# A tokenizer, state-space block and two MLPs on one core: norm factors straight from the variance, and another order at two turns

## The reference

```
h  = patches @ W.T + b
x  = layernorm(h)
m  = rmsnorm(x) * rms1_w ; zxbcdt = m @ in_proj.T       # z, x, B, C, dt
dt = softplus(dt_in @ dt_proj.T + bias)
h_t = exp(dt*A) * h_{t-1} + dt*x*B ; y = sum_n C*h_t    # 1024 channels, 16 states
y  = (y + D*x) * silu(z)
x1 = x + y @ out_proj.T
x2 = x1 + MLP(rmsnorm(x1) * rms2_w)
h  = h + x2 ; out = h + MLP2(layernorm(h))
```

## Time and profile before

| | |
|---|---|
| median of 3 executions | 671.52 us (671.13 to 671.97) |
| the profiled execution | 673.53 us |
| its span | 671.7 us |
| PE busy | 631.7 us (94%) |
| DVE busy | 417.6 us (62%) |
| POOL busy | 429.2 us (64%) |
| ACT busy | 345.1 us (51%) |
| mean granted clock of PE | 0.98 |

### The profile page before, as it was taken

One profiled execution on the slowest core, in us unless ns is written; L12 is line 12 of the kernel. 1 busy time (PEld: TensorE's weight loads), 2 busy tenths in 40 slices (PEclk: granted clock), 3 DMA queues, 4 the chain that ended last, 5 costly groups with the idle time before them and its releaser, 6 DMA issues.

```text
span 671.7 us, 8616 instructions
## 1 busy us (share of the span) xinstructions
PE 631.7 (94%) x2846; PEld 504.8 (75%) x2846; DVE 417.6 (62%) x532; ACT 345.1 (51%) x772; POOL 429.2 (64%) x244
## 2 busy tenths in 40 slices
PE   4959998799999899999998999999999999999998
PEld 3737765466666667777765777766999998999998
DVE  4077896889887889878898988850322223332132
ACT  4359789348888564334365433422543442653441
POOL 0176874527877999997879987644464463445461
PEclk9878998899999899999999999999999999999999
DMA  8699998369999959999967999534443353244421
GB/s 340 236 358 348 311 303 301 137 211 365 344 363 351 392 198 346 414 354 320 334 257 259 387 343 335 180 121 132 134 143 126 125 158 126 63 128 137 143 68 44
DMA packets 49165, 163.50 MB, mean 243 GB/s; under 512 B 4321, under 2 KB 18529, under 8 KB 48481
## 3 DMA queue, kind: packets, MB, share of 16 engines
q1 hardware_dynamic: 49120, 162.95, 69.5%
HBM read 145.24 MB, written 17.69 MB: 243 GB/s over the span
## 4 chain that ended last, share of the span: by engine, by line
PE 77%; DVE 12%; ACT 4%; issue 3%; DMA 2%; POOL 1%; SPq 0%; DVEq 0%; ACTq 0%
PE work L1001 55%; PE da L1001 15%; PE work L1011 6%; DVE da L790 6%; DVE hs L800 2%; ACT L525 1%; DMA bb<-b_rows 1%; ACT da L551 1%; DMA c_rows<-c_rows 1%; DMA sm<-small 1%; DVE sq L872 1%; DVE a L855 0%; POOL hs L450 0%; DVE sq L888 0%; DVE a L881 0%
## 5 line engine op out<-in xcount | busy, mean ns | idle before, releaser
L790 DVE TENSOR_TENSOR_SCAN da<-da,hs 128x580 f32<-128x580 f32 (+1 forms) x128 | 191.1, 1493 | 42.8 <-POOL hs L450 25.8
L450 POOL TENSOR_TENSOR hs<-dtx,bb 128x1160 f32<-128x1160 f32 (+1 forms) x64 | 171.2, 2677 | 63.6 <-PE work L1011 54.5
L429 POOL TENSOR_TENSOR ws<-wraw,ws 128x1024 fp32r<-128x1024 f32 x40 | 101.4, 2535 | 92.9 <-ACT ws L560 92.9
L1001 PE MATMUL work<-sq,wraw 128*128 128x290 f32 x512 | 127.0, 407 | 4.2 <-DVE gate L941 2.6
L1001 PEld LDWEIGHTS work<-sq,wraw 128*128 128x128 f32 x512 | 96.1, 189 | 34.8 <-issue 5.2
L1001 PE MATMUL work<-hn,win 128*128 128x290 f32 (+1 forms) x336 | 105.7, 465 | 16.8 <-DVE hn L863 8.1
L551 ACT ACTIVATE da<-dt,a_neg 128x261 f32<-128x261 f32 (+1 forms) x256 | 118.2, 493 | 0.0
L800 DVE TENSOR_TENSOR hs<-da,cb 128x580 f32<-128x580 f32 (+1 forms) x128 | 105.3, 823 | 10.4 <-DMA cb<-c_rows 2.5
L1001 PEld LDWEIGHTS work<-hn,win 128*128 128x128 f32 x336 | 66.8, 203 | 51.2 <-issue 27.1
L548 ACT COPY da<-zeros 128x58 f32<-128x58 f32 (+1 forms) x128 | 27.6, 216 | 125.7 <-DVE hs L800 125.5
L560 ACT CAST ws<-wraw 128x1024 fp32r<-128x1024 f32 x48 | 50.3, 1049 | 70.3 <-PE da L1001 34.4
(11 more groups left out here) (98 smaller groups left out, 649.3 us busy)
## 6 DMA issues: line engine op xcount, KB each, us to landing
wraw<-w_stream SPq DMA_DIRECT2D x104, 512.0 KB, 4.1
bb<-b_rows SPq DMA_DIRECT2D x32, 700.0 KB, 7.9
cb<-c_rows SPq DMA_DIRECT2D x32, 700.0 KB, 5.9
bb<-b_rows SPq DMA_DIRECT2D x32, 580.0 KB, 8.3
cb<-c_rows SPq DMA_DIRECT2D x32, 580.0 KB, 6.3
c_rows<-c_rows SPq DMA_DIRECT2D x8, 875.0 KB, 10.6
c_rows<-c_rows SPq DMA_DIRECT2D x8, 725.0 KB, 6.8
win<-w_in SPq DMA_DIRECT2D x4, 1024.0 KB, 13.0
```

What stands on the lines that cost most here:

```text
L429: nc.gpsimd.tensor_tensor(ws[:, k % NW, 1, :], wraw[:, split_loads[k] % NRAW, :], ws[:, k % NW, 0, :].bitcast(F32), ALU.subtract).then_inc ...
L450: nc.gpsimd.tensor_tensor(hs[:, u % NH, 0:NQ * n].rearrange("p (n t) -> p n t", t=n), dtx[:, t % 2, 0:n].unsqueeze(1).to_broadcast([P, NQ, ...
L790: nc.vector.tensor_tensor_scan(da[:, j, 0:w], da[:, j, 0:w], hs[:, u % NH, j * w:(j + 1) * w], 0.0, ALU.mult, ALU.add).then_inc(scan_done, 1)
L1001: last = nc.tensor.matmul(dst, w, x, start=(k == 0), stop=(k == len(pairs) - 1))
```

## The change

1. **Norm factors.** The RMS norm of the layer norm's output has the mean square var/(var+eps). With eps added and both roots taken together, the factor on the centred token is 1/sqrt(var (1+eps) + eps^2). ACT computes this first, as Exp(-0.5 Ln((1+eps) var + eps^2)), into the mean's bank, and DVE makes `hn` at once from the centred `a`. Then ACT computes the layer norm's own factor, and DVE scales `a` in the step `rms1`. The Exp to 1/(var+eps) and the DVE product on the variance are gone, and two semaphores with them.
2. **Tokens of chunk 1.** `tokc` becomes four steps `tok`. Their squares go, for chunk 1, into `th` and `acc` instead of `sq`; so the waits for `xs(0,7)` and for the stores of B move from the tokens to the steps that write `sq`. `in_z(0,7)` moves from slot 13 to slot 11; `in_c`, `dtp` and `xs` of tile 7 share slot 12, tokens go to slot 13, mean and variance to 14, `in_dt` and the first `in_b` to 15, and all of chunk 1's tiles come two slots sooner.
3. **Turn of the chunks.** `dtp(1,6)` and `xs(1,6)` come in slots 30 and 31, slot 32 is empty. In slots 30 to 32 PE does the state sum before the other steps, and sum(31) directly after sum(30). The last gate of chunk 0 comes in the middle of unit 33 on DVE instead of behind it.

```diff
-    slots = [(None, [("bmean", 0), ("tokc", 0), ("mean", 0), ...
+    slots = [(None, [("bmean", 0), *tokens(0), ("mean", 0), ...
...
-    bg += [[("dtp", 0, 7), ("in_c", 0, 7)], [("xs", 0, 7), ("in_z", 0, 7)]]
-    bg += [[("tokc", 1)], [("mean", 1), ("ln1", 1)], [("rms1", 1)], [("in_dt", 1), ("in_b", 1, 0)],
-           [("in_x", 1, 0), ("in_b", 1, 1)], [("in_x", 1, 1)]]
+    bg[-1].append(("in_z", 0, 7))
+    bg += [[("in_c", 0, 7), ("dtp", 0, 7), ("xs", 0, 7)], tokens(1), [("mean", 1), ("ln1", 1)],
+           [("rms1", 1), ("in_dt", 1), ("in_b", 1, 0)], [("in_x", 1, 0), ("in_b", 1, 1)], [("in_x", 1, 1)]]
     bg += two_tiles(1, 0) + two_tiles(1, 2) + two_tiles(1, 4)
     bg[-1].append(("in_z", 1, 6))
+    bg += [[("dtp", 1, 6)], [("xs", 1, 6)]]
-    first = [[("dtp", 1, 6), ("xs", 1, 6)], [("xs", 1, 7)], o[0:2], o[2:4]]
+    first = [[], [("xs", 1, 7)], o[0:2], o[2:4]]
...
+        def token_square(c, k):
+            if c == 0:
+                return sq[:, k, 0:TS[c]]
+            return (th[:, k, :] if k < 2 else acc[:, (k - 2) * TM:(k - 1) * TM])[:, 0:TS[c]]
...   (ACT, ln1)
-                    link(nc.scalar.activation(ln, bank(s), ACT.Ln, bias=eps_ap))
-                    nc.scalar.activation(inv, ln, ACT.Exp, scale=-1.0).then_inc(inverse_done, 1)
-                    act.wait_ge(h_done, KD * (c + 1))
-                    nc.scalar.activation(bank(("mean", c)), ln, ACT.Exp, scale=-0.5).then_inc(rstd_done, 1)
+                    link(nc.scalar.activation(both, bank(s), ACT.Ln, scale=1.0 + EPS, bias=eps_square))
+                    act.wait_ge(h_done, KD * (c + 1))
+                    nc.scalar.activation(bank(("mean", c)), both, ACT.Exp, scale=-0.5).then_inc(rstd_done, 1)
+                    link(nc.scalar.activation(ln, bank(s), ACT.Ln, bias=eps_ap))
+                    nc.scalar.activation(bank(s), ln, ACT.Exp, scale=-0.5).then_inc(rstd_done, 1)
...   (ACT, rms1)
-                    act.wait_ge(scaled_var, c + 1)
-                    link(nc.scalar.activation(rstd[:, 0:n], bank(var), ACT.Ln, bias=eps_ap))
-                    nc.scalar.activation(bank(var), rstd[:, 0:n], ACT.Exp, scale=-0.5).then_inc(rstd_done, 1)
+                    return
...   (ACT, in_dt, in_x, in_b)
+                    if c >= 1 and kind == "in_x":
+                        full(act, ("xs", c - 1, KI - 1))
+                    if c >= 1 and kind == "in_b":
+                        act.wait_ge(b_stored, 16 * 2 * c)
+                    if c >= 1 and kind == "in_dt":
+                        full(act, ("dtp", c - 1, KI - 1))
...   (DVE: ln1 now makes hn, rms1 scales a)
-                    nc.vector.tensor_tensor(bank(s), bank(s), rstd[:, 0:n], ALU.mult).then_inc(scaled_var, 1)
...   (DVE, order of a slot)
-                        parts.append(("gate", unit // QU - 1))
+                        parts.insert(2 if unit == UNITS + 1 else len(parts), ("gate", unit // QU - 1))
...   (PE, order of a slot)
-                n = 0 if unit is not None and unit % QU == 1 else (len(steps) + 1) // 2
+                n = 0 if unit is not None and (unit % QU == 1 or UNITS - 2 <= unit <= UNITS) else (len(steps) + 1) // 2
                 for s in steps[:n]:
                     step(s)
                 if unit is not None and 2 <= unit <= UNITS:
                     state_sum(unit - 2)
+                if unit == UNITS:
+                    state_sum(UNITS - 1)
                 for s in steps[n:]:
                     step(s)
-                if unit == UNITS:
-                    state_sum(UNITS - 1)
```

More of the change, by code:

```diff
@@ L90, in m_steps, with tokens @@
     return s
+def tokens(c):
+    return [("tok", c, k) for k in range(KD)]
 def outs(c):
@@ L104, in schedule @@
 def schedule():
-    slots = [(None, [("bmean", 0), ("tokc", 0), ("mean", 0), ("ln1", 0), ("rms1", 0), ("in_dt", 0), ("in_b", 0, 0), ("in_b", 0, 1),
+    slots = [(None, [("bmean", 0), *tokens(0), ("mean", 0), ("ln1", 0), ("rms1", 0), ("in_dt", 0), ("in_b", 0, 0), ("in_b", 0, 1),
                      ("dtp", 0, 0), ("in_c", 0, 0), ("in_x", 0, 0), ("xs", 0, 0)]),
@@ L166, in work_bank_uses @@
                 ring = RINGS[2]
-            names = {"tokc": [("tokc", s[1], k) for k in range(KD)], "rms1": [],
-                     "gu": [(s, "gate"), (s, "up")]}.get(s[0], [s])
+            names = {"rms1": [], "gu": [(s, "gate"), (s, "up")]}.get(s[0], [s])
             for n in names:
@@ L221, in build @@
         acc = sb("acc", [P, 2 * TM])
-        cols = sb("cols", [P, 8])
+        cols = sb("cols", [P, 9])
         zeros = sb("zeros", [P, 2 * TM // STEPS])
         eps_ap, w_sum, b_mean, minus_one, tok_bc = (cols[:, 0:1], cols[:, 1:2], cols[:, 2:3], cols[:, 3:4], cols[:, 4:8])
+        eps_square = cols[:, 8:9]
         with ExitStack() as scanned:
@@ L597, in step @@
                 n = TS[s[2] if kind in ("squares", "root") else c]
-                if kind == "tokc":
-                    if c == 0:
+                if kind == "tok":
+                    k = s[2]
+                    if (c, k) == (0, 0):
                         act.wait_ge(tokb_done, 1)
[L601 to L609, removed]
+                    full(act, s)
+                    nc.scalar.activation(a(c, k), bank(s), ACT.Identity, bias=tok_bc[:, k:k + 1]).then_inc(centered, 1)
+                    nc.scalar.activation(token_square(c, k), bank(s), ACT.Square,
+                                         bias=tok_bc[:, k:k + 1]).then_inc(free_of(s), 1)
@@ L610, in step @@
                 elif kind == "ln1":
-                    v, ln, inv = NORMS.index(s), rstd_ln[:, 0:n], rstd[:, 0:n]
+                    ln, both = rstd_ln[:, 0:n], rstd[:, 0:n]
                     log_tables()
-                    if v >= 1:
-                        act.wait_ge(norm_done, KD * v)
                     full(act, s)
+                    link(nc.scalar.activation(both, bank(s), ACT.Ln, scale=1.0 + EPS, bias=eps_square))
+                    act.wait_ge(h_done, KD * (c + 1))
+                    nc.scalar.activation(bank(("mean", c)), both, ACT.Exp, scale=-0.5).then_inc(rstd_done, 1)
@@ L770, in _ @@
             nc.vector.memset(minus_one, -1.0)
+            nc.vector.memset(eps_square, EPS * EPS)
             nc.vector.memset(zeros[:, :], 0.0)
@@ L850, in step @@
                 elif kind == "ln1":
-                    dve.wait_ge(inverse_done, c + 1)
-                    nc.vector.tensor_tensor(bank(s), bank(s), rstd[:, 0:n], ALU.mult).then_inc(scaled_var, 1)
-                    dve.wait_ge(rstd_done, NORMS.index(s) + 1)
+                    v, both = NORMS.index(s), ("mean", c)
+                    dve.wait_ge(rstd_done, v + 1)
+                    if c >= 1:
+                        full(dve, ("in_z", c - 1, KI - 1))
+                        full(dve, ("in_c", c - 1, KI - 1))
                     for k in range(KD):
-                        nc.vector.tensor_tensor(a(c, k), a(c, k), bank(("mean", c)), ALU.mult).then_inc(norm_done, 1)
+                        nc.vector.scalar_tensor_tensor(out=hn[:, k, 0:n], in0=a(c, k), scalar=small_ap(S_W1, k),
+                                                       in1=bank(both), op0=ALU.mult, op1=ALU.mult).then_inc(norm_done, 1)
+                    dve.wait_ge(norm_done, KD * (v + 1))
+                    dve.sem_inc(free_of(both), 1)
                 elif kind == "rms1":
@@ L858, in step @@
                     dve.wait_ge(rstd_done, v + 1)
-                    if c >= 1:
-                        full(dve, ("in_z", c - 1, KI - 1))
                     for k in range(KD):
-                        dve.wait_ge(norm_done, KD * (v - 1) + k + 1)
-                        nc.vector.scalar_tensor_tensor(out=hn[:, k, 0:n], in0=a(c, k), scalar=small_ap(S_W1, k),
-                                                       in1=bank(var), op0=ALU.mult, op1=ALU.mult).then_inc(norm_done, 1)
+                        nc.vector.tensor_tensor(a(c, k), a(c, k), bank(var), ALU.mult).then_inc(norm_done, 1)
                     dve.wait_ge(norm_done, KD * (v + 1))
                     dve.sem_inc(free_of(var), 1)
-                    dve.sem_inc(free_of(("mean", c)), 1)
                 elif kind == "rms2":
@@ L1050, in step @@
                     product(s, [(mean_w[:, :], sm[:, S_TOKB:S_TOKB + KD])], KD)
-                elif kind == "tokc":
+                elif kind == "tok":
                     pe.wait_ge(pat_loaded, 16 * (c + 1))
                     pe.wait_ge(tokw_done, 1)
-                    for k in range(KD):
-                        product(("tokc", c, k), [(tokw[:, k * P:(k + 1) * P], pat[:, OFF[c]:OFF[c] + n])])
+                    product(s, [(tokw[:, s[2] * P:(s[2] + 1) * P], pat[:, OFF[c]:OFF[c] + n])])
                 elif kind == "mean":
@@ L1058, in step @@
                 elif kind == "ln1":
-                    product(s, [(mean_w[:, :], sq[:, k, 0:n], free_of(("tokc", c, k)), uses[("tokc", c, k)][1] + 1)
```

(3 more changed lines are left out.)

3 lines of the change are left out of this document (removed).

## The result

| | before | after |
|---|---|---|
| median | 671.12 us (6 executions) | 664.73 us (6 executions) |
| ratio, 95% interval | | 0.9918 (0.9899 to 0.9938) |
| profiled execution | 673.53 us | 665.30 us |
| its span | 671.7 us | 663.5 us |

The change makes the kernel 6.4 us faster by the medians, 5.5 us by the ratio, with an interval of 4.2 to 6.8. The forecast was 10.0 us, 661.5. In the profiled executions it is 8.2 us. The difference between 8.2 and 6.4 lies mostly in the profiled execution of the kernel before: it took 673.53 us, while its executions in this study's four comparisons, 65 in all, have medians between 670.3 and 671.1 us.

The account below looks back on a forecast made before the run. TensorE (PE) was taken as three quarters of the chain of waits, its idles before full stretches paid in full. Turn 7.85, norm 1.84 and clock 0.3 gave 10.0 us: 673.5 to 663.5 profiled, median 661.5, range 657 to 668.

Parts of the forecast that it names:

- Part 1: First norm: a shorter chain from Ln to the first `hn` lets PE start 1.84 us sooner.
- The 0.3 for the clock: Behind the first norm's shorter gap, PE's clock may stay up, worth 0.3 us.
- Every step is a chain of dependent work: From the first norm on, the 1.84 us saved is carried through to the next turn.
- Part 2: Second chunk's tokens and norm sooner: unit 32 starts at 203.6 instead of 206.29, worth 2.7 us ahead of the turn.
- the 13.3 us of earlier `in_dt`: Second norm: PE starts `in_dt` at 117.0 instead of 130.28; 5.9 us of this is sums put behind it.
- The forecast of slower: Rival, chance 0.06: held-back sums free `hs` buffers late, costing 12.6 us against 10 gained, so 674.1 us.
- the larger last group of gates: On ACT, before unit 32: 1.3 us added to the time of the 14 units from 18.
- Part 3: Turn of the chunks: sums 30 and 31 first and gate 7 earlier, so `out(0,0)` starts at 212.3 instead of 221.65.
- I take 1.5: Turn: allowance of 1.5 us for unit 33's late `cb` load, between nothing and 7.0 us.
- Two signs of being wrong: Wrong if DVE waits for `cb` or POOL for `bb` in units 30 to 34, or gaps bring back half clock.
- I had taken 2.0 off for both: Whole kernel: the median taken as 2.0 us below the profiled time, giving 661.5 from 663.5.
- the loads set the turn: Rival, chance 0.13: unit 33's `cb` lands no sooner except by the norm's 1.84; gain 4.2 us, so 667.3.

Follow-up runs that it names:

- the run with chunk 0's norm alone: Kernel before with the new norm for chunk 0 only, chunk 1 keeping the old norm: 669.37 us, ratio 0.9978.
- the weights in slot 30: Changed kernel with its six first weight loads issued in slot 30, as before, instead of slot 28: 663.91 us, ratio 0.9899.
- one by one: Changed kernel with its six first weight loads in slots 29, 31, 33, 34, 35 and 36 instead of together in slot 28: 662.21 us, ratio 0.9873.
- the short norm alone: Kernel before with only the new norm factors, in both chunks; tokens, slots and turn as before: 665.90 us, ratio 0.9929.
- the slots alone: Kernel before with only the second chunk's earlier slots; both norms and the turn's orders as before: 677.47 us, ratio 1.0109.
- the short norm in the old slots: Kernel before with new norm, turn's orders and weight loads spread over slots 29 to 36: 660.96 us, ratio 0.9854; without the spreading 665.18 us.

## Why the prediction came out as it did

**Part 1, the chain.** Right to a few hundredths: 1.65 us from Ln to PE against 1.67, and 1.5 us of time in the run with chunk 0's norm alone against 1.84. The 0.3 for the clock was too little for the profile that the sum started from: there the clock's part is 7.79 - 6.10 = 1.7 us. The clock fell behind the old first gap in three of four profiles and behind the new one in none of ten. "Every step is a chain of dependent work" held only in part, since behind the norm the rows of B go out to DRAM and come back as `bb`. In the runs with the weights in slot 30 and one by one, which are alike up to there, that store was issued at 17.93 and 19.93 us, and unit 1's scan began at 38.29 and 38.26: POOL stood 5.01 us for its first `bb` in the one and 3.10 in the other. So 2 us of lead at the norm can be gone by unit 1. How much of the start's lead lasts to the end is open as well, since the run of chunk 0's norm, 6.5 us ahead at the output product, is 4.4 ahead at the end of its span.

**Part 2.** The sum was good as a description of the changed kernel. Shifted by the 4.1 us by which this execution was ahead at unit 12, it gives 103.6 for gate 2 (measured 104.2), 112.9 for `in_dt` (113.7) and 131.0 for unit 18 (131.8). It was wrong as an account of what earns it. I priced slots and second norm together and wrote the 13.3 us of earlier `in_dt` down to the slots. The runs show that the short norm alone reaches the same lead at unit 20 (8.3 against 8.2), that the slots alone lose 7.3 us, and on top of the norm nothing is gained. The forecast of slower, by sums that are held back, named a real mechanism. It decides when the norm is long: POOL then stood 12.97 us for sum(13). In the changed kernel only gate 2's wait for sum(11) is left of it, 2.58 us, where the sum had 2.4. And ACT had too small a price: the sum took 1.3 us for the larger last group of gates, but with the loads out of the way unit 32 is 2.9 us less ahead than unit 31.

**Part 3.** The multiply, the gate and the output product follow each other as forecast. The step that failed is "I take 1.5" for the loads. Measured by moving the weights it is 3.5 us at the output product: 213.46 against 209.95. My argument was that the landing would move with the weights. It took 184.84 to 200.4, still 15.5 us, but it now hit unit 31, whose multiply is due sooner than unit 33's. I had looked at the one load that was late before, not at which load would be next in line behind the bunch. PE's idle before the output product was 7.1 us, not 3 to 5, for the same reason. Two signs of being wrong that the prediction named did come: the waits for `cb` and `bb` in units 31 and 32, and the half clock behind the gap.

**The terms side by side,** as leads over the kernel before's profile in us. The last row is the changed kernel with its weights one by one.

```
             start to unit 12   to unit 32   to the output product   sum
forecast           2.1              2.7          5.2                10.0
changed kernel     4.1             -1.0          5.1                 8.2
weights late       4.0              0.9          6.8                11.7
```

The 5.2 is 6.7 less the 1.5 for the loads. From unit 32 on, the sum without loads was right to 0.1 us. Up to unit 32 it was 3.7 us too high: 1.9 for the loads, which hit there already, and 1.8 mostly for ACT. The start was 1.9 us better than forecast, of which the clock behind the first gap explains up to 1.7. So the 10.0 came as near to 8.2 as it did partly by luck: errors of +1.9 and -3.7 stood against each other.

**From the profile to the median.** Of the 8.2 us, 6.4 are in the medians. The profiled execution of the kernel before was 2.4 us above its median and that of the changed kernel only 0.6; I had taken 2.0 off for both. The half clock at the second norm is not to blame, since every profile with the long second norm has it. Half-clock stretches that not all of the other profiles of this schedule share lie behind the first norm, at 51.0 to 54.4 us and under the token products at 112.4 to 115.8 us. Which of them made this execution slow is not shown.

**The rest.** The lead was kept from the output product to the end, as said. The rival "the loads set the turn" gave a gain of 4.2 us and was nearer to the measured 6.4 than the forecast of 10.0. It had the right place and the wrong unit.

## What to carry over

A faster step upstream makes every buffer free sooner, so look through the DMA queue for what is issued in a bunch and what stands directly behind it; spreading six loads over the slots in which they are needed was worth 2.5 us here by the medians, 1.4 in the old kernel and 4.2 with the short norm in the old slots. Price each part against a kernel with and without the others: the slots lose 7 us with the long norm and nothing to speak of with the short one. And before a gain is read from one profile, see which of its slow stretches other profiles of nearly the same kernel have as well.

## What was not expected of the hardware

Idle time of PE in front of a full stretch cost more than itself. At the turn 2.6 us more idle (9.65 against 7.09) put 6.0 instead of 3.9 us of the output product at half clock, 1.0 us of time on top.

Half clock cost nothing where PE did not set the pace. Between 33 and 47 us the changed kernel's profile has 9.6 us of matmul time at half clock and the kernel before's 3.5, and the lead is 4.1 us at unit 1 and 4.1 at unit 12.

And the start varies from execution to execution. Unit 1's scan began at 39.98 to 42.32 us in four profiles with the old norm, and at 37.66 to 38.97 in ten with the new one. The earliest of the four is the one in which the clock stayed up behind the first gap.
